# A gated cross-attention block on one core: Q stored untransposed and read by a transposing DMA transfer

## What is computed

```python
x = x + tanh(g_xattn) * xattn(layernorm(x), ctx, Wq, Wk, Wv)
x = x + tanh(g_ffn) * ffn(layernorm(x), w1, w2, w3)
# xattn: 32 heads of 32; q and k are RMS-normalised by head
q = rmsnorm(heads(x @ Wq.T)); k = rmsnorm(heads(ctx @ Wk.T)); v = heads(ctx @ Wv.T)
out = softmax(q @ k.T * 32 ** -0.5) @ v
# ffn: weights are rounded to -1, 0 or 1 by their mean absolute value
hidden = sigmoid(x @ quant(w1).T) * (x @ quant(w2).T); y = hidden @ quant(w3).T
```

## Time and profile before

| | us |
|---|---|
| three executions, median (lowest to highest) | 2405.26 (2403.8 to 2405.95) |
| the profiled execution, its own time | 2409.68 |
| its span, first to last instruction | 2407.9 |
| PE busy in the span | 2338.2 (97%) |
| DVE busy | 1423.5 (59%) |
| ACT busy | 1373.6 (57%) |
| POOL busy | 895.3 (37%) |
| transposes of Q on PE (L1388), busy in total | 17.3 |
| copies of them, ACT (L838) and DVE (L1112) | 16.5 and 11.7 |

### The profile page before, as it was taken

How to read it: one execution, slowest core, us unless ns; L and a number is a source line. 1 busy time by engine, 2 the same in 40 slices (tenths; PEclk the granted TensorE clock), 3 DMA queues, 4 the chain that set the end, 5 groups by cost and what they waited for, 6 DMA issues and landing times.

```text
span 2407.9 us, 46736 instructions
## 1 busy us (share of the span) xinstructions
PE 2338.2 (97%) x17618; PEld 1367.3 (57%) x17618; DVE 1423.5 (59%) x2346; ACT 1373.6 (57%) x2894; POOL 895.3 (37%) x857
## 2 busy tenths in 40 slices
PE   7998899999999999999999999889999999999999
PEld 5885465566656566666666565555555555544444
DVE  5666677776776777777767767664353444410000
ACT  4875787788888888888888888751111111110000
POOL 3664255565655656565656556430000000000000
PEclk9999999999999999999999999999999999999999
DMA  7785544465535445544545454554232323244351
GB/s 244 232 271 172 139 114 99 104 129 100 125 93 124 106 102 125 113 102 113 131 100 124 93 100 105 129 159 125 94 114 95 114 95 104 79 136 147 103 166 53
DMA packets 383233, 299.16 MB, mean 124 GB/s; under 512 B 276512, under 2 KB 338464, under 8 KB 382496
## 3 DMA queue, kind: packets, MB, share of 16 engines
q1 hardware_dynamic: 383008, 296.17, 46.8%
HBM read 196.22 MB, written 49.55 MB: 102 GB/s over the span
## 4 chain that ended last, share of the span: by engine, by line
PE 33%; POOL 29%; issue 26%; DVE 1%; DMA 1%; POOLq 1%; ACT 1%; DVEq 0%; SPq 0%; ACTq 0%
PE ps L1447 21%; POOL krs L707 14%; PE ps L1563 11%; POOL oinv L725 5%; POOL kms L702 4%; POOL osum L723 2%; POOL osum L730 2%; POOL oinv L727 1%; POOL ca L737 1%; POOL cn L751 1%; POOLq L60 0%; POOL crs L747 0%; DMA wraw<-in_wffn 0%; ACT pf L958 0%; DMA stage<-x_normalised 0%
## 5 line engine op out<-in xcount | busy, mean ns | idle before, releaser
L1479 PE MATMUL ps<-wk,cpair 128*128 128x512 f16 x4608 | 1116.5, 379 | 15.1 <-DVE cpair L1086 7.6
L1274 DVE TENSOR_TENSOR plo<-pf,phi 125x448 f16<-125x448 f32 x768 | 526.9, 687 | 160.8 <-ACT phi L949 158.4
L1479 PEld LDWEIGHTS ps<-wk,cpair 128*128 128x128 f16 x4608 | 393.7, 97 | 392.6 <-DVE cpair L1086 8.7
L958 ACT ACTIVATE pf<-ps 125x448 f32<-125x448 f32 x768 | 417.6, 544 | 145.1 <-PE ps L1501 137.1
L1447 PE MATMUL ps<-xnTh,w12q 128*128 128x512 f16 (+1 forms) x1408 | 478.9, 354 | 2.9 <-issue 2.1
L1447 PE MATMUL ps<-xnTl,w12q 128*128 128x512 f16 (+1 forms) x1408 | 478.6, 353 | 0.0
L949 ACT ACTIVATE phi<-pf 125x448 f16<-125x448 f32 x768 | 445.5, 580 | 8.5
L707 POOL TENSOR_TENSOR krs<-kms,mhalf 125x8 f32<-125x8 f32 x192 | 331.4, 1726 | 15.1
L702 POOL TENSOR_TENSOR kms<-kss,keps 125x8 f32<-125x8 f32 x192 | 95.5, 497 | 556.3 <-DVE kss L1240 556.3
L1525 PE MATMUL ps<-val,phi 125*128 125x65 f16 x3072 | 279.6, 192 | 18.9 <-DVE plo L1274 18.8
L1501 PEld LDWEIGHTS ps<-qT,kst 128*125 128x125 f16 x1536 | 209.2, 138 | 144.9
(11 more groups left out here) (113 smaller groups left out, 2461.0 us busy)
## 6 DMA issues: line engine op xcount, KB each, us to landing
gbuf<-in_wffn SPq DMA_DIRECT2D x66, 512.0 KB, 5.0
wraw<-in_wffn SPq DMA_DIRECT2D x66, 512.0 KB, 5.7
cstream<-in_ctx SPq DMA_DIRECT2D x48, 500.0 KB, 4.6
craw<-in_ctx SPq DMA_DIRECT2D x48, 500.0 KB, 4.6
hid<-hidden SPq DMA_DIRECT2D x7, 2816.0 KB, 12.7
hidden<-hh SPq DMA_DIRECT2D x66, 256.0 KB, 2.1
qT<-q_pairs SPq DMA_DIRECT2D x256, 56.0 KB, 2.2
wkraw<-in_wkv SPq DMA_DIRECT2D x4, 2048.0 KB, 8.9
```

Of the source, the lines that this page charges most:

```text
L958: act.activation(pf[0:KW, e % 6, :], bank(3 + e % 3)[0:KW, 0:2 * S], ACT.Exp, bias=LN128, scale=SCALE).then_inc(p_ready, 1)
L1274: dve.tensor_tensor(plo[0:KW, e % 6, :, :], pf[0:KW, e % 6, :].rearrange("p (t n) -> p t n", t=2), phi[0:KW, e % 6, :, :], ALU.subtract).t ...
L1479: mm = pe.matmul(bank(pt)[:, :], cpair[:, n % RING, a, kc, :], wkp[g][:, w, kc, :], start=(kc == 0 and m == 0), stop=(kc == KC - 1 and m = ...
```

## The change

The high and low parts of a half are now written twice each, side by side, so that a head takes 4 x 32 columns of `qnat`: high, high, low, low. This is done by broadcasting `qhat` over a new axis of length 2 in the same two instructions that made the parts before. `save_q` writes that tile as it stands, tokens in rows, to the DRAM tensor `q_stacked`, one transfer for each half, as soon as the low part is there. `q_stack`, `half_out` and the tile `qTs` are gone on all engines, and the last two halves need no place in unit 0. `load_qT` is one transposing transfer of 224 tokens by 8 heads x 128 columns. `half_high` of half h now waits until the save of half h - 2 has landed (`q_saved`), because it overwrites that tile. The two small sums that `q_stack` held (`w_sum`, `ctx_sums`) moved to `step_a` of PE.

```diff
-        qnat = sb(pa, "qnat", [P, 2, 16, 2, DH], F16)
-        qTs = sb(pa, "qTs", [P, 2, 2 * NP, P], F16)
+        qnat = sb(pa, "qnat", [P, 2, 16, 4, DH], F16)
...
-            def save_q(h, i, c):
-
-                sp.wait_ge(qTa_ready, h + 1)
-                sp.wait_ge(qTb_ready, h + 1)
-                for g in range(2):
-                    sp.dma_start(qst_d[2 * c + g, :, :, i * P:i * P + P].rearrange("p r t -> r p t"),
-                                 qTs[:, c, NP * g:NP * g + NP, :]).then_inc(q_saved[c], 16)
+            def save_q(h):
+
+                i, c = h // 2, h % 2
+                sp.wait_ge(qlo_ready, h + 1)
+                sp.dma_start(q_d[i * P:i * P + P, 16 * c:16 * c + 16, :, :].rearrange("t h a d -> t (h a d)"),
+                             qnat[:, c, :, :, :].rearrange("p h a d -> p (h a d)")).then_inc(q_saved[c], 16)
...
                 for c in range(2):
-                    if i:
-                        save_q(2 * i - 2 + c, i - 1, c)
+                    if 2 * i + c:
+                        save_q(2 * i + c - 1)
                     for n in stream_tiles(i + 1, c):
                         load_stream(n)
...
-                for i in range(4):
-                    for s in range(2):
-                        r0 = HD2 * s + DH * (i // 2)
-                        sp.dma_start(qT[DH * i:DH * i + DH, par, s:HG:2, :],
-                                     qst_d[g, :, r0:r0 + DH, b * S:b * S + S].rearrange("p r t -> r p t")
-                                     ).then_inc(q_in[par], 16)
+                sp.dma_start_transpose(qT[:, par, :, :], q_d[b * S:b * S + S, HG * g:HG * g + HG, :, :].rearrange(
+                    "t h a d -> t (h a d)")).then_inc(q_in[par], 16)
...
             def half_high(h, c):
                 act.wait_ge(qhat_ready, h + 1)
-                wait(act, qT_ready, h - 1)
-                act.activation(qnat[:, c, :, 0, :], qhat[:, :, :], ACT.Copy).then_inc(qhi_ready, 1)
...
-                act.activation(qTs[:, c, 0:NP, :], bank(4 + 2 * c, F16).rearrange("p (h n) -> p h n", n=P)[:, 0:NP, :],
-                               ACT.Copy).then_inc(qTa_ready, 1)
+                wait(act, q_saved[c], 16 * (h // 2))
+                act.activation(qnat[:, c, :, 0:2, :], qhat[:, :, :].unsqueeze(2).to_broadcast([P, 16, 2, DH]), ACT.Copy
+                               ).then_inc(qhi_ready, 1)
...
             def half_low(h, c):
                 dve.wait_ge(qhi_ready, h + 1)
-                dve.tensor_tensor(qnat[:, c, :, 1, :], qhat[:, :, :], qnat[:, c, :, 0, :], ALU.subtract
+                dve.tensor_tensor(qnat[:, c, :, 2:4, :], qhat[:, :, :].unsqueeze(2).to_broadcast([P, 16, 2, DH]),
+                                  qnat[:, c, :, 0:2, :], ALU.subtract
                                   ).then_inc(qlo_ready, 1)
...
-                for n in range(2 * NP):
-                    b = 4 + 2 * c + n // NP
-                    mm = pe.transpose(bank(b, F16)[:, (n % NP) * P:(n % NP) * P + P],
-                                      qnat[:, c, 2 * n:2 * n + 2, :, :].rearrange("p h a d -> p (h a d)"), identh[:, :])
-                mm.then_inc(qT_ready, 1)
...
                     q_half(2 * i + c, i, par, c, first)
-                    if not first:
-                        q_stack(2 * i - 2 + c, c, W_A_SUMS.get(i) if c == 0 else None, chunk_at(i) if c == 0 else None)
+                    if c == 0:
+                        wait(pe, cfr_ready, sum(n < i for n in CHUNK_STEPS))
+                        wait(pe, wfr_step, 2 * sum(n < i for n in W_A_SUMS))
+                        if i in W_A_SUMS:
+                            w_sum(W_A_SUMS[i], bank(5)[:, 304:304 + WQ])
+                        if chunk_at(i) is not None:
+                            ctx_sums(chunk_at(i))
                     if c == 0 and (not last or last == NT - 2):
                         x_transpose(i + 1)
```

More of the change, by code:

```diff
@@ L63, in flamingo_kernel @@
 def flamingo_kernel(nc, x_d, ctx_d, wq_d, wkv_d, wffn_d, gates_d, out_d):
-    qst_d = nc.dram_tensor("q_pairs", [G, NP, P, TOK], F16, kind="Internal").ap()
+    q_d = nc.dram_tensor("q_stacked", [TOK, NH, 4, DH], F16, kind="Internal").ap()
     cn_d = nc.dram_tensor("x1_normalised", [TOK, 2, D], F16, kind="Internal").ap()
@@ L214, in flamingo_kernel @@
         qms_ready = sem("qms_ready"); qrs_ready = sem("qrs_ready"); qhat_ready = sem("qhat_ready")
-        qhi_ready = sem("qhi_ready"); qlo_ready = sem("qlo_ready"); qT_ready = sem("qT_ready")
-        qTa_ready = sem("qTa_ready"); qTb_ready = sem("qTb_ready")
+        qhi_ready = sem("qhi_ready"); qlo_ready = sem("qlo_ready")
         q_saved = [sem(f"q_saved{i}") for i in range(2)]
@@ L371, in flamingo_kernel @@
         GATE_STEPS = sorted([(u, r) for u in range(U) for r in (15, 23)] + [(4, 11), (5, 11)])
-        Q_TAIL = ((0, 1, 2), (1, 6, 7))
-        def q_tail(k, r, step):
-            if k:
-                return []
-            return [c for c, pe_step, out_step in Q_TAIL if r == (pe_step if step == "stack" else out_step)]
         def phase_b_over(eng):
@@ L440, in _ @@
             load_ctx(3)
-            save_q(2 * NT - 2, NT - 1, 0)
             load_ctx(4)
             load_ctx(5)
-            save_q(2 * NT - 1, NT - 1, 1)
+            save_q(2 * NT - 1)
             for c in range(2):
-                sp.wait_ge(q_saved[c], 32 * NT)
+                sp.wait_ge(q_saved[c], 16 * NT)
             def load_w(j, s):
@@ L845, in step_a @@
                     half(h, c)
-                    if not first:
-                        half_out(h - 2, i - 1, c)
                     if c == 0 and (not last or last == NT - 2):
@@ L900, in value_high @@
                                        ACT.Copy, scale=cvf[0:KW, nb:nb + 1]).then_inc(v1_ready, 1)
-                    for c in q_tail(k, r, "out"):
-                        half_out(2 * NT - 2 + c, NT - 1, c)
                     if j == 0 and behind(k, t, 1):
@@ L1373, in q_half @@
                 mm.then_inc(q_ready, 1)
-            def q_stack(h, c, w=None, n=None):
-                pe.wait_ge(qlo_ready, h + 1)
-                wait(pe, qTa_ready, h - 1)
-                wait(pe, qTb_ready, h - 1)
-                if c == 0:
-                    wait(pe, cfr_ready, sum(i < h // 2 + 1 for i in CHUNK_STEPS))
-                    wait(pe, wfr_step, 2 * sum(i < h // 2 + 1 for i in W_A_SUMS))
-                if w is not None:
-                    w_sum(w, bank(5)[:, 304:304 + WQ])
-                if n is not None:
-                    ctx_sums(n)
-                for n in range(2 * NP):
-                    b = 4 + 2 * c + n // NP
-                    mm = pe.transpose(bank(b, F16)[:, (n % NP) * P:(n % NP) * P + P],
-                                      qnat[:, c, 2 * n:2 * n + 2, :, :].rearrange("p h a d -> p (h a d)"), identh[:, :])
-                mm.then_inc(qT_ready, 1)
             x_transpose(0)
@@ L1482, in unit_b @@
                             mm.then_inc(kv_ready, 1)
-                    for c in q_tail(k, r, "stack"):
-                        q_stack(2 * NT - 2 + c, c)
                     if attends(k, r, SHIFT):
@@ L1495, in unit_b @@
                         if e == 0:
-                            pe.wait_ge(q_in[ap], 128 * ((u - 1) // 2 + 1))
+                            pe.wait_ge(q_in[ap], 16 * ((u - 1) // 2 + 1))
                         if not (k == 1 and e < 3):
```

11 lines of the change are left out of this document (removed).

## The result

| | before | after |
|---|---|---|
| median on the same chip, us (executions) | 2405.61 (4) | 2427.42 (4) |
| lowest to highest | 2403.8 to 2408.2 | 2425.88 to 2429.76 |
| the profiled execution: own time, span | 2409.68, 2407.9 | 2428.2, 2426.4 |
| `qhat` of half 2 to `qhat` of half 27 | 164.80 | 189.01 |

The ratio is 1.0091, with a 95% interval from 1.0073 to 1.0108: the changed kernel is 21.8 us slower. The direction was forecast, but the size was not: 7.8 us were expected, and 2427.4 lies above the range. In the profiled executions the span grew by 18.5 us: that of the kernel before stood 4.1 us above its median (2409.68 - 2405.61), that of the changed one 0.8.

The account below looks back on a forecast made before the run. It took phase A as bound by a loop of ACT, DVE and POOL, nearly tied with PE; +7.3 us there and +0.5 into phase B gave +7.8, a median of 2413.1 us, range 2407 to 2420.

Parts of the forecast that it names:

- The loop of ACT, DVE and POOL: Phase A, from one `qhat` to the next without PE: 6.26 us a period, growing to 6.70 with the change.
- ACT's wider copy: High part of Q on ACT, in the loop: 1024 columns instead of 512 add 0.44 us a period.
- PE's 12 us: 28 batches of Q transposes leave PE, 0.43 us each, 12.0 us in all; all of it turns into waits for `qhat`.
- The transposing read: Reading Q in phase B as one 224 x 1024 transpose: lands in 5.4 us, hidden by phase B.
- The way into phase B: After `qhat` of half 27: wider high part +0.44, low part +0.54, last Q transposes gone -0.43; +0.5 us.
- the one on the copies of ACT and DVE: Phase A: the removed copies (590 ns on ACT, 418 ns on DVE) lie outside the loop and give nothing by themselves.
- (a): First halves of steps 6 and 7, DVE making low parts of weights ahead of `qhat`: 1.25 us late each.
- (b): Other first halves, DVE row without weights: some eight made about 0.05 us late, 0.4 us in sum.
- The clock: Phase A: PE's granted clock stays 1.00 despite new idle gaps; a fall there would show the forecast wrong.
- The loop grows little: Rival, phase A: ACT's second write costs under 0.3 us, time within 0.2% of before, 2402 to 2410; chance 0.14.
- The saves land late: Rival: Q saves landing past 9.9 us delay the halves; 12 us throughout gives +26, 2439 us; chance 0.10.
- PE was the limit: Rival, phase A: PE set the pace, so all 12.0 us of transposes are saved, 2393.3 us; chance 0.08.

Follow-up runs that it names:

- e2: Changed kernel with ACT writing the high part of Q once, its second place left zero: 2415.04 us, phase A 178.32 us.
- e1: Changed kernel with DVE writing the low part of Q once (512 columns), the save still 512 KB: 2413.04 us, phase A 176.07 us.
- e4: Changed kernel with an added DVE copy of 512 columns out of PSUM between sums and low part in every half: 2410.27 us.
- e9: Kernel before with one more DVE subtraction out of SBUF ahead of the low part, second halves only: 2410.06 us.
- e10: Kernel before with one more DVE copy out of PSUM ahead of the low part, second halves only: 2406.51 us.
- e3: Changed kernel with DVE's low part written as two subtractions of 512 columns: 2415.51 us, phase A 179.39 us.
- e6: Changed kernel with Q read by 8 transposing transfers a unit in place of one: 2571.63 us, ratio 1.0679 to the kernel before.
- e12: Kernel before with the DVE copy to `qTs` moved ahead of the low part: 2406.87 us, ratio 0.9998.
- e11: Changed kernel with DVE reordered, `xn` kept ahead of `qhat`, and the second high part copied by ACT outside the loop: 2394.18 us, ratio 0.9947 to the kernel before.
- e5: Changed kernel with DVE reordered (PSUM reader before the low part, `xn` behind `qhat`), POOL's x work later, one copy added: 2405.98 us, ratio 0.9999 to kernel before.

## Why the prediction was wrong in size

**What held.** The loop of ACT, DVE and POOL that the prediction found in the earlier trace rows does set phase A after the change. ACT's wider copy is in it at its price (forecast 0.44, e2 shows 0.43 in each period). PE's 12 us, and what the loop grew, turned into waits for `qhat`: 31.2 us in 21 waits, against 5.2 in 2 before. ACT never waited for a save, and a save lands in 3.4 us. The transposing read lands in 4.9 us (forecast 5.4), and phase B hides it. The way into phase B cost 0.6 us (forecast 0.5).

**The step that failed** is the one on the copies of ACT and DVE, that "the trace puts both behind the squares and the sums, outside the loop, so they give nothing by themselves", with its counterpart in (a) and (b), that the low part costs something only where DVE itself is late. Both took the durations of POOL, 0.60 and 2.92 us, as fixed. They are mostly its own, but in part DVE's. Two terms are missing from the period:

- The addition is held until the low part ends: +0.54 with the wider one, in all 25 periods, 13.5 us. e1 takes 12.9 off.
- The copy on DVE was what kept the next reader of SBUF from the start of the power: +0.43 in 11 second halves, where that is `xn`, and +0.36 and 0.37 in halves 25 and 26, where it is a low part of weights (`wk`), 5.5 us. e4, e9 and e10 show it from both sides.

The copy and what followed it before the change, beside the power of the earlier trace rows that began at 141.68:

```profile
141.44 0.42 DVE L1112 COPY qTs<-ps 128x512 f16<-128x512 f16 x1
141.78 0.81 DVE L1012 TENSOR_SCALAR xn<-xraw,bag,xrs 128x1024 f32<-128x1024 f32 x1
```

`xn` came 0.10 us too late to hold it.

So 6.26 + 0.43 + 0.54 = 7.23 for first halves and 7.66 for second, where 7.22 and 7.65 were measured. Over the phase, 25 periods of the old loop are 156.5 us, and with 10.8, 13.5 and 5.5 us they come to 186.3. What lies above that (weights, the context tile) is 2.7 us, where the prediction had kept 4.6: part of what was late on DVE is hidden in the longer periods (0.71 us in each of the two steps with weights, where 1.25 was forecast). The sum is 189.0.

**What was left out ahead of phase A's steady part.** The prediction left everything before half 2 as it was, and the two profiles seem to agree, with that `qhat` at 46.06 us in both. But e9 and e10, which are the kernel before up to half 3, have it at 43.8, and e1 to e4 at 44.6 to 44.9. From 20 to 46 us the granted clock is 0.87 in the profile of the kernel before, and 0.93 in e9 and e10 and after the change. So up to some 2 us of the 21.8 may lie there; one profile of each doesn't settle it.

**What was left out at the other end.** The prediction gave phase B its old length. It got about 6 us shorter (2.0 between 376 and 480 us, 4.3 near the end). A likely cause is that the one transposing read is issued in 1.6 us in the case shown, where 8 plain transfers took 3.9 (at 349.46 before), so the gates' weights behind it in SP's row come earlier. e6 shows that the issues of this read can set when those weights arrive. The kernels with the new read in one transfer all regain 1.3 to 3.1 us between 376 and 480 us, and 2.2 to 3.2 between 1434 and 1546; e9, e10 and e12 with the old read regain at most 0.1 and 0.5. So these two parts, 5.2 us in the changed kernel, go with the new read, though that the queue is their cause was only argued. The last 1.1 us, from 1546 to 1639, stay open: e12 with the old read regains 1.6 there too, and stretches of PE at 1.2 GHz lie elsewhere in the traces (from 1540 to 1660 us the granted clock is 0.90 before and 0.91 after).

**The clock.** It didn't stay at 1.00 in phase A: the window from 112.3 to 145.4 us has 0.90. PE had idle gaps ahead of every half by then. It cost nothing that the period shows, since PE waited for `qhat` in any case, 28.02 us busy of 33.10.

**The rivals.** "The loop grows little" falls with e2. "The saves land late" falls with e1 to e4, which keep the bytes. "PE was the limit" was wrong for the time, but nearer than I took it. In the steady steps of the kernel before, PE starts its halves 5.99 and 6.83 us apart by turns, 6.41 in the mean, 0.15 over the loop. e10 and e12 have these same two numbers, though e10 takes 0.37 off the loop in second halves: phase A lost 0.85 us there, not 13 x 0.37 = 4.8. So PE did set the steady pace, by 0.15 a period, and its time could not come back because the loop stood right behind. In e11, with both shortened, PE's halves are 5.54 and 6.24 apart, 5.89 in the mean, and the loop is 5.88. The saving on PE was real, and 6.3 us of it and of the shorter loop show in phase A; it needed an order in which nothing holds POOL.

**Could it be read beforehand?** The rows were there. In the earlier trace rows the addition of 16 columns takes 0.60 us, and DVE's low part (0.68) starts directly behind the sums, as the addition does. The still smaller `vep` of the same trace (128 x 1) takes 0.19 us at 138.30 and 0.58 at 124.73. Phase B, which the change doesn't touch, has the same sign 140 times: the addition `kms` of 8 values a row takes 0.20 us where DVE runs nothing, and 0.51 to 0.66 in all 140 cases that start beside DVE's `plo`, a subtraction out of SBUF. Two durations of one small form are a sign to look for who runs beside it. The Trainium skill ("SBUF — State Buffer", Who interferes with whom) says it: a DVE instruction with two SBUF inputs contends with a GpSimd instruction that reads SBUF, and so does one-operand work in a two-port mode such as `tensor_scalar`, while `tensor_reduce` on trn2 never does. The trace agrees on all three: 1.13 us beside the low part, 3.34 beside `xn`, and no hold by sums (in phase B of the kernel before, `oinv` takes its 0.20 us in all 22 cases that start beside a `TENSOR_REDUCE` out of SBUF). I had not weighed that rule.

## What to carry to other kernels

Before a duration of POOL goes into a sum as a constant, look what DVE runs at its start: here subtractions with two operands out of SBUF and the `tensor_scalar` of `xn` held it to their end, and instructions that read PSUM didn't. A removed instruction can have been the gap that kept two others apart, so ask of each deletion what now stands next to what. A saving on an engine that ties with a loop is only worth something together with an edit that shortens the loop: here the change alone gave +0.9%, and with a new order on DVE and one copy moved out of the loop -0.5%.

## What the runs showed of the hardware

- POOL is held only at the start of an instruction. Its power of 16 columns runs its 2.91 us beside a whole low part of 1.22 us (e4) or beside `xn` that starts 0.10 us behind it (before), but takes 3.24 to 3.34 when DVE's instruction out of SBUF is already under way, and 3.99 beside one that starts 0.01 us behind it (e5). What a hold adds is what DVE's instruction has left at POOL's start, less some 0.15 us: 0.58 left gives 0.43 (`xn`, after), 0.55 gives 0.40 (e12), 0.48 gives 0.33 (e3), 1.23 gives 1.08 (e5), and for the addition 1.05 gives 0.91 (after). DVE isn't slowed in return: the low part is 1.22 us with the power under way.
- The page of the Trainium skill named above says that whoever issues first has the shared ports for the whole instruction, and the other is fully blocked. Where DVE is first the runs agree; where POOL's power is first they don't.
- A write of 2 x 512 columns from 512 broadcast ones costs as 1024 columns on both engines: 1.06 us on ACT and 1.22 on DVE, against 0.63 and 0.68 for 512.
- Eight transposing transfers of 224 x 128 are issued in 10.68 us, or 1.3 each (e6), and one of 224 x 1024 in 1.56 (after). Here splitting a transpose cost the queue by the number of transfers much more than by their size.
